# Loading x's first block over ScalarE's DMA queue instead of SyncE's

## The reference, cut to what matters

```
h = gelu(embedding @ W0 + b0); h = gelu(h @ W1 + b1)
att = softmax(h @ W2 + b2)
agg_w = einsum('bk,koi->boi', att, weight);  agg_b = att @ bias_k
hid = einsum('boi,bih->boh', agg_w, x) + agg_b[:, :, None]
shared = (relu(hid @ up_w) ** 2) @ down_w
routed = ((hid @ fc1_w) @ expert_w) * sum(top_k(hid @ gate_w, 2)) @ fc2_w
out = x + layernorm(shared + routed, gamma, beta)
```

## Time and profile before

| what | value |
|---|---|
| time, median of 3 runs | 256.61 us (256.14 to 256.63) |
| span of the profiled execution | 254.6 us |
| PE busy | 248.0 us (97%) |
| DVE, ACT, POOL busy | 155.8, 81.8, 39.4 us |
| all DMA | 15.60 MB |
| chain that ended last, by engine | PE 89%, DMA 3%, issue 2%, DVE 1% |

### The profile page before, as it was taken

The page is one execution under the profiler, slowest core; times in us unless marked ns, Lnnn a source line. Parts: engine busy times, 40 slices in busy tenths (PEclk is TensorE's granted clock), DMA queues, the critical chain, the costliest instruction groups (busy, mean ns, idle before and its releaser), DMA issues.

```text
span 254.6 us, 3526 instructions
## 1 busy us (share of the span) xinstructions
PE 248.0 (97%) x1291; PEld 207.1 (81%) x1291; DVE 155.8 (61%) x272; ACT 81.8 (32%) x142; POOL 39.4 (15%) x45
## 2 busy tenths in 40 slices
PE   8999999999999999999999999999999999999992
PEld 7877887988888888888888888888888888788891
DVE  4798999944448964644447983464444953406453
ACT  4669856411003452321112534331111355202100
POOL 2400021000117120001114411001111700001110
PEclk9999999999999999999999999999999999999997
DMA  6994804001111400001111220000011100000111
GB/s 161 332 324 153 305 17 153 0 0 44 41 41 41 167 0 0 3 0 42 41 41 41 78 87 0 0 0 11 31 41 44 42 0 0 0 3 8 74 44 41
DMA packets 10444, 15.60 MB, mean 61 GB/s; under 512 B 1088, under 2 KB 4928, under 8 KB 10432
## 3 DMA queue, kind: packets, MB, share of 16 engines
q1 hardware_dynamic: 9984, 15.33, 17.6%
q10 hardware_dynamic: 448, 0.11, 0.2%
HBM read 11.23 MB, written 4.20 MB: 61 GB/s over the span
## 4 chain that ended last, share of the span: by engine, by line
PE 89%; DMA 3%; issue 2%; DVE 1%; SPq 1%; ACT 0%; POOL 0%; POOLq 0%; DVEq 0%
PE ps L932 27%; PE ps L934 27%; PE ps L933 27%; PE ps L906 4%; DMA late<-in_up_w_dram 3%; PE ps L998 2%; PE ps L950 1%; PE ps L956 1%; PE ps L952 1%; SPq L322 0%; POOL rstd L417 0%; DVE stats L714 0%; DVE y_buf L712 0%; DVE h_full L636 0%; ACT h_hi L474 0%
## 5 line engine op out<-in xcount | busy, mean ns | idle before, releaser
L932 PE MATMUL ps<-down_hi,sq_hi 128*128 128x512 f32 (+1 forms) x136 | 51.2, 377 | 0.0
L933 PE MATMUL ps<-down_lo,sq_hi 128*128 128x512 f32 (+1 forms) x136 | 51.2, 377 | 0.0
L934 PE MATMUL ps<-down_hi,sq_lo 128*128 128x512 f32 (+1 forms) x136 | 51.2, 376 | 0.0
L932 PE MATMUL ps<-h_hi,up_hi 128*128 128x512 f32 x120 | 46.8, 390 | 0.0
L934 PE MATMUL ps<-h_hi,up_lo 128*128 128x512 f32 x120 | 46.7, 389 | 0.0
L933 PE MATMUL ps<-h_lo,up_hi 128*128 128x512 f32 x120 | 46.7, 389 | 0.0
L417 POOL TENSOR_TENSOR rstd<-mv,half 128x1 f32<-128x1 f32 x16 | 15.3, 954 | 158.2 <-DVE mv L719 153.2
L512 ACT ACTIVATE relu_sq<-ps 128x512 f32<-128x512 f32 x32 | 19.1, 597 | 57.7 <-PE ps L934 44.3
L712 DVE TENSOR_TENSOR y_buf<-ps,y_buf 128x512 f32<-128x512 f32 x15 | 10.4, 692 | 41.0 <-PE ps L934 40.7
L685 DVE CAST sq_hi<-relu_sq 128x512 fp32r<-128x512 f32 x32 | 22.6, 706 | 16.2 <-ACT relu_sq L514 15.7
L932 PEld LDWEIGHTS ps<-down_hi,sq_hi 128*128 128x128 f32 x136 | 25.6, 188 | 4.7
(11 more groups left out here) (137 smaller groups left out, 308.7 us busy)
## 6 DMA issues: line engine op xcount, KB each, us to landing
out_dram<-late SPq DMA_DIRECT2D x15, 256.0 KB, 2.0
x_cur<-in_x_dram SPq DMA_DIRECT2D x3, 1024.0 KB, 5.2
late<-in_down_w_dram SPq DMA_DIRECT2D x4, 512.0 KB, 5.3
late<-in_up_w_dram SPq DMA_DIRECT2D x3, 512.0 KB, 8.8
x_cur<-in_x_dram SPq DMA_DIRECT2D x2, 512.0 KB, 7.2
experts_sb<-in_experts_dram SPq DMA_DIRECT2D x3, 256.0 KB, 3.5
agg_b<-aggb_dram SPq DMA_DIRECT2D x1, 768.0 KB, 4.9
latents_sb<-in_latents_dram SPq DMA_DIRECT2D x1, 528.0 KB, 4.8
```

The lines of the kernel that those rows point to most:

```text
L932: nc.tensor.matmul(dst, a_hi, b_hi, start=first, stop=False)
L933: nc.tensor.matmul(dst, a_hi, b_lo, start=False, stop=False)
L934: return nc.tensor.matmul(dst, a_lo, b_hi, start=False, stop=last)
```

## The change

The two loads of x's first block move from SP's queue to ACT's. The first stands behind the warming activation L438, the second behind the first layer's Gelu L441. The small load of `bias_sb` moves the other way, from ACT's queue to SP's, ahead of the experts' loads. Nothing else changes: the bytes, the shapes, the semaphores and all waits on them are the same.

```diff
@@ block.sync
             sp.dma_start(b2_rows[:, :], kernels[0, C * C + C:C * C + C + K].partition_broadcast(NB)
                          ).then_inc(b2_loaded, 16)
+            sp.dma_start(bias_sb[:, :], kernels[0:K2, C * C:]).then_inc(bias_loaded, 16)
             for m in range(LC):
                 sp.dma_start(experts_sb[:, m, FIRST], experts_v[:, m, FIRST]).then_inc(experts_loaded[m], 16)
             sp.dma_start(experts_sb[:, :, REST], experts_v[:, :, REST]).then_inc(experts_loaded[LC], 16)
-            sp.dma_start(x_cur[:, 0:2, :], x_v[:, 0:2, :]).then_inc(first_x_loaded, 16)
-            sp.dma_start(x_cur[:, 2:TB, :], x_v[:, 2:TB, :]).then_inc(x_loaded, 16)
@@ block.scalar
             act.dma_start(mlp_sb[:, NB + D:], mlp[:, NB + D:]).then_inc(mlp_loaded[1], 16)
-            act.dma_start(bias_sb[:, :], kernels[0:K2, C * C:]).then_inc(bias_loaded, 16)
             act.wait_ge(dve_const, 2)
             nc.scalar.activation(warm[:, :], warm[:, :], ACT.Gelu).then_inc(warmed, 1)
+            act.dma_start(x_cur[:, 0:2, :], x_v[:, 0:2, :]).then_inc(first_x_loaded, 16)
             act.wait_ge(mlp_loaded[1], 16)
             act.wait_ge(h1_done, 1)
             nc.scalar.activation(hid1[:, :], H1[:, 0, :], ACT.Gelu, bias=b0_sb).then_inc(gelu_done, 1)
+            act.dma_start(x_cur[:, 2:TB, :], x_v[:, 2:TB, :]).then_inc(x_loaded, 16)
             act.wait_ge(h2_done, 1)
```

## The result

The changed kernel took 259.24 us (259.04 to 259.45), against 256.62 (256.14 to 256.71) for the kernel before: the ratio is 1.0108, with a 95% interval from 1.0095 to 1.0122. It is slower, by 2.6 us, where 2.1 were forecast. That number needs one remark at once: run again in two further measurements, the same kernel gave 257.16 and 258.79 as medians. Its executions fall into two levels, from 256.9 to 257.5 and from 258.7 to 259.6, and the first measurement had met the upper level four times out of four.

What follows compares the result with a forecast made beforehand. PE was taken to bound the kernel, busy 97% of the span, so only prologue delay counts. Mixing 2.2 us late less 0.1 took the span from 254.6 to 256.7; a 2.0 offset gave 258.7 us, range 256.3 to 261.0.

Steps and rivals of the forecast that it cites:

- the 2.1 of the sum: Whole kernel: mixing 2.2 us late, less about 0.1 saved, lengthens the profiled span from 254.6 to 256.7 us.
- When x is issued: ACT's queue in the prologue: first x load issued at 1.8 us, during the table load; second at about 3.9.
- Sharing: Prologue loads: x and experts in two queues share bytes equally; experts 0 complete at 5.9 or 6.4, rest at 10.8.
- landing marks: Prologue loads before the change, KB moved by landing time: 256 at 5.1 us, 512 at 5.9, 768 at 7.6, 1280 at 10.1, 1792 at 11.5.
- Which load binds: PE's second expert fold waits for the rest of the experts, landing at 10.8 us; experts 1 at 8.8 delay less.
- The sum of +2.2 for the late mixing: PE's mixing start: 10.8 + 1.85 folding + 0.4 for L902 gives 13.05 us against 10.83.
- its own signs of being right: Changed profile: x issued at 1.8, experts' rest landing 10 to 11.5 as second fold starts, L912 about 13, L950 about 17.4.
- The tie at L636: DVE's bias addition waits on mixing and up weights within about 0.1 us, so earlier `up_w` wins at most 0.15.
- Late issue: ACT's queue: first x load issued only at 3.2 us, experts' rest lands at 9.7; 257.6 us, chance 0.23.
- stretched issue: ACT's queue: full queue stretches second x issue to 1.4 us, 0.5 beyond the free 0.9, hidden; no separate chance.
- The experts keep their lead: Prologue loads: SP's older work is served first, experts' rest lands by 8.65; 256.5 us, no change, chance 0.18.

## Why the prediction was right, and where not

The direction, the size within 0.6 us and the place were right: the prologue, the experts' loads, PE's fold, a shift that nothing gives back. The number owes much to luck. Of the 2.6 us measured, 1.4 are a late clock that the forecast had in no such form. Where the clock mostly rose in time, the change cost 0.6 us (257.16 against 256.55), far below the 2.1 of the sum though inside the range. Point by point:

*When x is issued.* Right. L449's early start was the right row to read: the first x load went out at 1.76 (1.8 forecast), during the table load, and the second at 3.90 (3.9). Its issue took 0.42 us and held nothing up; L443 starts at 5.15 as before. The rule of the Trainium skill, "TensorE: Matmul & The Clock Gate", section "Architectural detail: the array is 16× 32×32, not 1× 128×128", on ScalarE's queue is borne out in so far as the sequencer is ahead of the engine. How deep the queue is, no run shows.

*Sharing.* This step failed, and its result came out near by luck. It read the earlier trace rows as two queues in competition, and took equal shares. The rows fit as well with service in the order of issue: ACT's small loads had been issued at 0.74 and 1.18, the experts at 1.79. The run that holds the queues fixed and moves the issue (x behind L440), and the one that holds the order and takes the second queue away (x first in SP's queue), decide for the order. The forecast's own landing marks come near the first profile with it. Experts 0 are complete when x's 512 KB and their own 256 have moved, at the 768 KB mark, 7.6 (measured 7.79); experts 1 at 1024, 8.8 (8.5); the rest at 1280, 10.1 (9.9). The prediction had 6.4, 8.8 and 10.8. But in the two later profiles they landed at about 7.2, 7.9 and 9.0, so the marks fit the first profile partly by chance.

Two readings under the marks were off. They are not the KB moved: at 256 GB/s from 3.0 to 7.6 us the engines moved some 1180 KB, not 768, so x was already moving before the experts' rest had landed. And the premise that the engines are full from 3 us on did not hold with x in front: from 3 to 4 us they moved 12 GB/s, and 69 and 30 in the two later profiles, against 186 before. With one queue and x in front it was 21, so the slow start goes with x's load and not with the second queue; why, no run shows. The experts' issue was moved by 0.63 us (1.79 to 2.42) and not by 0.51, as the `bias_sb` issue took 0.57 us on SP.

*Which load binds.* Hence the wrong member was named. The forecast had the rest of the experts at 10.8 and the second fold waiting for it. The rest landed at 9.9, 1.6 us before its turn; it was the first load, at 7.79 against 6.14, that PE waited for. The sum of +2.2 for the late mixing stands against 1.69 from the wait in that execution and 1.1 to 1.2 in the two profiled later. So of its own signs of being right, the second fold starting as its data land did not come true in any profile, and L912 stood at 13.91 and then at 11.90 and 11.98 where about 13 was forecast.

*The tie at L636.* Right: `up_w` was issued 0.55 us earlier and brought nothing. L636 now waits 0.24 us for the mixing, as one would read from the 13.54 and 13.69 of the kernel before.

*The rivals.* Late issue and stretched issue did not occur. "The experts keep their lead" names the right quantity but not the condition: they keep it when they are issued first, as the run with x behind L440 shows (256.83, against 256.5 for that rival).
*The sum by the corrected steps.* The fold late by 1.1 us, less the 0.1 at the tie, on the medians of before (256.3 to 256.6): 257.3 to 257.6. The two profiled executions of the lower level took 257.43 and 257.41; the others go down to 256.86, and no profile shows what they save. With the fold late by 1.69 and the late clock's 1.40, as in the first profile: 3.0 more, 259.3 to 259.6, measured 259.33. The 258.7 on record lay between these sums, at the lower edge of the upper level.

What stays open: by what the order of issue is kept across two queues, since the runs show only that it is, and not to the letter; why x's load begins so late; why some executions of the upper level lie more than 1.4 us above the lower one; and what besides a gap puts off the clock's rise, since one measurement of the same kernel had the upper level four times of four and another once in twelve. No version tried is faster than the kernel before.

## What to carry to other kernels

Moving a load to another engine's queue also changes its place in the order of issue, and here the order decided who waits: list all issues of all queues by time, and let no large load go ahead of one that is due sooner. An issue written behind an activation or a table load goes out when its waits are met, not when the engine is done; to hold it back, a wait on something late has to stand ahead of it. A gap opened in PE's prologue, before its clock has risen, can cost its own length and a late clock on top, so look for two levels in the single times before believing a median, and judge the early clock by the spacing of the matmuls.

## What the runs showed of the hardware

- Large loads of two queues were served nearly in the order of their issue. With x issued at 3.91 and the experts by 3.78, ACT's queue moved nothing from 4 to 6 us while SP's moved 0.66 MB. Where two issues overlapped in time or nearly so, the queues ran side by side, and then by packets and not by bytes. In the changed kernel from 8.5 to 9.5 us, x's second load (issued at 3.90, packets of 2 KB) beside `up_w`'s (from 3.83 on, 512 B) and the last of the experts' rest (1 KB, from 3.35 on):

```profile
q10 hardware_dynamic: 150, 0.31, 79.7%
q1 hardware_dynamic: 159, 0.09, 28.8%
```

  The page "DMA: Bandwidth & Descriptors" of the Trainium skill, section "Queues, rings and completion order", says that each engine takes turns between its rings packet by packet. That agrees with these two rows (150 packets against 159). It does not agree with the rows of 4 to 5 and 4 to 6 us above, where both queues had loads issued and one of them moved next to nothing.
- A load of 2 KB issued 0.36 us behind a load of 512 KB of the other queue landed 6.8 us later; where it was issued ahead of x it took 2.5 to 4.7, the 4.7 in the changed kernel's first profile (issued at 1.19, x at 1.76). So the order of issue is not kept to the letter. Nor was it for large loads close together: in the changed kernel's second profile x's second load, issued at 4.43, moved beside `up_w`'s first from 7.5 us on, whose issue had ended at 4.30.
- The first fold's eight entries took 1.83 us at PE's full clock and 3.23 with the first six of them at the half (1.2 GHz against 2.4 by their spacing), and there were two levels, their nearest executions 1.2 us apart, in three kernels: the changed one (9 of 21 executions in the upper), the one with x first in SP's queue (5 of 10), and the one with a wait alone (5 of 10). With idle matmuls in the gap none of 17 executions in three kernels was in the upper level.
